# A graph network on one core: VectorE, not GpSimd, puts the next block's gather indices in place

## What is computed

```
k, q, v = typed_linear(x, ntype, Wk / Wq / Wv)          # one of 3 matrices by the node's type
a  = sum(att[etype] applied to k[src] * q[dst]) * pri / sqrt(32)      # per edge and head (4 heads of 32)
w  = softmax of a over the edges with the same dst
h  = segment_sum(msg[etype] applied to v[src] * w, dst)
x  = typed_linear(h, ntype, Wa) * alpha + x * (1 - alpha)
```

## Time and profile before

| | |
|---|---|
| time, median of 3 runs | 7933.0 us (7932.73 to 7936.94) |
| span of the profiled execution, first to last instruction | 9921.5 us |
| gathers L443 | 4160, busy 3981.4 us, 957 ns each |
| copies L439 on POOL | 130, 219 ns each |
| busy share of the span: PE, DVE, POOL, ACT | 56%, 47%, 46%, 41% |

### The profile page before, as it was taken

How to read it: one execution, slowest core, us unless ns; L and a number is a source line. 1 busy time by engine, 2 the same in 40 slices (tenths; PEclk the granted TensorE clock), 3 DMA queues, 4 the chain that set the end, 5 groups by cost and what they waited for, 6 DMA issues and landing times.

```text
span 9921.5 us, 147395 instructions
## 1 busy us (share of the span) xinstructions
PE 5554.4 (56%) x33354; PEld 4735.9 (48%) x33355; DVE 4643.5 (47%) x12764; ACT 4066.5 (41%) x10084; POOL 4557.4 (46%) x4797
## 2 busy tenths in 40 slices
PE   5654545586554555955555559445454594555554
PEld 3544444464444444744444447344444573444443
DVE  5254545532555555235554552355555523555555
ACT  1244444432444444324444443344444433444442
POOL 0345555433455554335555542445555424555553
PEclk9866676797677666977666679767767796676667
DMA  2322222213222221232222213222222132222221
GB/s 69 144 62 70 70 71 70 68 70 125 69 71 72 71 72 56 100 107 72 69 72 72 69 45 124 93 69 71 70 70 71 37 140 83 73 74 73 73 76 36
DMA packets 272656, 761.00 MB, mean 77 GB/s; under 512 B 87871, under 2 KB 104356, under 8 KB 271908
## 3 DMA queue, kind: packets, MB, share of 16 engines
q0 software_dynamic: 199680, 545.53, 19.2%
q1 hardware_dynamic: 72228, 208.51, 5.4%
HBM read 557.87 MB, written 195.88 MB: 76 GB/s over the span
## 4 chain that ended last, share of the span: by engine, by line
PE 31%; another core or an unknown queue 25%; DVEq 16%; issue 12%; DVE 10%; POOLq 3%; ACT 2%; ACTq 1%; DMA 0%; POOL 0%; SPq 0%
PE ps L535 6%; PE ps L627 6%; DVEq L1061 5%; DVEq L1051 5%; PE ps L643 4%; PE ps L648 4%; PE ps L552 3%; POOLq L459 3%; DVEq L228 2%; PE ps L555 2%; PE ps L588 1%; PE ps L642 1%; DVE prod L1045 1%; DVE wmsg L1025 1%
## 5 line engine op out<-in xcount | busy, mean ns | idle before, releaser
L443 POOL DMA_INDIRECT rows<-table,idx_now x4160 | 3981.4, 957 | 3529.5 <-DVE wmsg L1029 1878.9
L642 PE MATMUL ps<-zeros,identb 128*128 128x132 bf16 x2080 | 555.0, 267 | 3189.9 <-DVE wmsg L1029 2780.9
L704 ACT ACTIVATE prod<-iota_n,dloc 128x128 bf16<-128x128 f32 x6240 | 1988.9, 389 | 106.0 <-issue 78.7
L642 PEld LDWEIGHTS ps<-zeros,identb 128*128 128x128 bf16 x2080 | 242.1, 116 | 3353.3 <-issue 3171.5
L1045 DVE TENSOR_TENSOR prod<-ps,rows 128x512 f32<-128x512 f32 x1040 | 715.5, 688 | 2352.6 <-remote 1820.4
L709 ACT ACTIVATE ohf<-prod,ones 128x512 f32<-128x512 bf16 x1040 | 750.5, 722 | 2326.4 <-remote 1887.0
L627 PE MATMUL ps<-qn,ohT 128*128 x8320 | 1583.6, 350 | 67.8 <-issue 62.7
L627 PEld LDWEIGHTS ps<-qn,ohT 128*128 128x128 f32 x8320 | 1407.3, 255 | 135.9 <-issue 129.7
L643 PE MATMUL ps<-wmsg,ohf 128*128 128x132 f32 x4160 | 1267.6, 398 | 0.0
L648 PE MATMUL ps<-wmsg,ohf 128*128 128x132 f32 x4160 | 1090.9, 355 | 0.0
L588 PE MATMUL ps<-identb,oh 128*128 128x128 bf16 x4160 | 531.8, 268 | 730.4 <-ACT ohT L721 358.8
(11 more groups left out here) (162 smaller groups left out, 6391.4 us busy)
## 6 DMA issues: line engine op xcount, KB each, us to landing
table<-rows SPq DMA_DIRECT2D x245, 768.0 KB, 3.2
rows<-table,idx_now POOLq DMA_INDIRECT x4160
out<-h SPq DMA_DIRECT2D x1, 3072.0 KB
wk<-in_L_gnn_Wk SPq DMA_DIRECT2D x20, 48.0 KB
wq<-in_L_gnn_Wq SPq DMA_DIRECT2D x20, 48.0 KB
wv<-in_L_gnn_Wv SPq DMA_DIRECT2D x20, 48.0 KB
wa<-in_L_gnn_Wa SPq DMA_DIRECT2D x20, 48.0 KB
attw<-in_L_gnn_rel_att SPq DMA_DIRECT2D x20, 24.0 KB
```

What stands on the lines that cost most here:

```text
L443: pool.indirect_dma_start(out=rows[:, slot, j, :], out_offset=None, in_=table, in_offset=bass.IndirectOffsetOnAxis(ap=idx_now[:, half, c:c ...
L642: pe.matmul(bank[:, AW:2 * AW], identb[:], zeros[:], start=True, stop=True)
L704: act.activation(squares[:, turn % 2, j * P:(j + 1) * P], iota_n[:], ACT.Square, bias=dloc[:, at(4 * q + j)], scale=-1.0)
```

## The change

At the first quad of a layer POOL copies 64 columns, both halves of `idx_now`, and drains once. For blocks 2 to 25 VectorE copies the 32 columns: in slot 2 of block n, behind L1029, it writes those of block n+1 to the other half and raises a new semaphore `indices_ready`. POOL waits for that semaphore before the first gather of blocks 2 to 25. It is 24 copies a layer on DVE, 120 in all, and one copy with a drain a layer on POOL where there were 26.

```
@@ -180,6 +180,7 @@
         s_gath = [sem(f"gathered{i}") for i in range(RING)]
+        s_idx = sem("indices_ready")
@@ -435,9 +436,11 @@
                     half = slot // BQ
-                    if slot % BQ == 0:
-                        pool.tensor_copy(idx_now[:, half, :], idx[:, at(4 * q, BS)])
+                    if is_first(q):
+                        pool.tensor_copy(idx_now[:], idx[:, 0:2 * BS].rearrange("p (a c) -> p a c", a=2))
                         pool.drain()
+                    if slot % BQ == 0 and not is_first(q, RING):
+                        hold(pool, s_idx, l * (BLOCKS - 2) + n - 1)
                     for j in range(4):
                         c = 4 * (slot % BQ) + j
                         pool.indirect_dma_start(
@@ -1027,6 +1030,8 @@
                         dve.tensor_copy(wmsg[:, b, :, D:AW], w).then_inc(s_wm, 1)
+                    if slot % BQ == 2 and not is_first(n) and not beyond(n + 1, BLOCKS):
+                        dve.tensor_copy(idx_now[:, 1 - slot // BQ, :], idx[:, at((n + 1) * BS, BS)]).then_inc(s_idx, 1)
                     if b == 1 and not beyond(q + 2):
```

## The result

The changed kernel takes 7484.0 us (median of 4 runs, 7473.97 to 7490.11), the kernel before 7934.97 us (median of 4, 7932.73 to 7936.99). The ratio on record is 0.9428, with a 95% interval of 0.9417 to 0.9440 (the two medians alone give 0.9432). It is faster by 451 us, where 420 had been forecast. The profiled execution has a span of 7482.8 us, so this time profile and metric agree.

What follows compares the result with a forecast made beforehand. It took POOL's queue to bound the edge stages in timed runs. Per block -3.7 + 0.1 + 0.1 = -3.5 us, times 120 = -420, took 7933 to 7513, rounded to 7515 us; range 7450 to 7760.

Steps and rivals of the forecast that it cites:

- POOL's queue as the bound: Edge stages: in timed runs POOL's queue of gathers, copies and drains sets their time.
- 1188 us a layer: POOL's work in an edge stage: gathers 1046, boundaries 92, last gather to last weighting 50 us.
- the 1988.5 us: Profiled span over timed median, 9921.5 against 7933.0 us; put down to remote DVE waits absent from timed runs.
- 3.7 us a boundary: POOL at block boundaries: copy with drain delays the next gather by 3.7 us, 25 times a layer.
- 24 boundaries, since the first is covered: POOL per layer: the boundary into block 1 gains nothing, with 16 slots free; 24 gain, 120 in all, 444 us.
- 0.2 us a block held back: Loss per block: 0.1 us for lengthened gathers, 0.1 us for gathers and DVE waiting for each other.
- 1086 us a layer: DVE and PE chain in the edge stages: its low bound, with no remote waits.
- rival 1: DVE's chain takes over early, remote waits partly remaining: 7715 us, range 7570 to 7880, chance 0.22.
- The added copy: DVE, slot 2: 120 copies of 128x32 at 0.2 us, 24 us in all, beside the gathers while POOL bounds.
- the estimated 298 us: Port contention by the Trainium skill: 120 copies cost up to 298 us, result near 7810; the prediction doubted that size.
- What would show it: Signs: timed median falls about 420 us, profile span stays 9921 within 100, POOL's rest grows from 2038.1 to near 2450.
- its own sign: Whole profile: the prediction counts as wrong if the profile's span falls with the time.

Runs made afterwards that it cites:

- e1: The kernel before the change, unedited, profiled a second time: 7946.19 us, profile span 7944.4 us.
- e4: Changed kernel with a POOL drain put back at the boundaries into blocks 1 to 25 of each layer, copy left on VectorE: 7935.82 us, ratio 0.9989.
- e7: Changed kernel with three gathers a quad instead of four, zeros in the fourth place: 7085.36 us, ratio 0.8925.
- e3: Changed kernel with one POOL drain put back at the boundary into block 1 of each layer: 7499.85 us, ratio 0.9438.
- e6: Changed kernel with five index copies on VectorE instead of one, four into an unused tile: 7469.45 us, ratio 0.9407.
- e8: Changed kernel with L1032, the small copy of the weights, written as a product with ones: 7473.63 us, ratio 0.9412.
- e10: Changed kernel with softmax weights read from PSUM, so L1028 has one input there, and L1007 dropped: 10081.44 us, ratio 1.0178, on chip 14.
- e9: Changed kernel with L1028 split into four operations of 128x128: 10086.36 us, ratio 1.0181, on chip 14.
- e11: Changed kernel with two POOL drains in a row at the 125 boundaries: 9867.75 us, ratio 0.9959, on chip 14.
- e2: The changed kernel, unedited, run again on chip 13: 7485.76 us, ratio 0.9422.
- e5: Changed kernel with the 120 copies back on POOL, a block ahead, with a semaphore and no drain: 7490.61 us, ratio 0.9431.

## Why the prediction was right, and where it was not

**POOL's queue as the bound.** Right. The account of 1188 us a layer for POOL's work against 1190.7 was the step that carried it; in e1 the five stages have a mean of 1193 us, and POOL never waits over 0.3 us for a slot. That the sum came so close is in part luck: the mean gather is 970 ns and not 957, some 11 us a layer more, and from the last gather to the last weighting it is 43.5 us and not 50 (7735.9 to 7779.4 in e1). e4 and e7 show it by experiment: POOL's time put back comes back whole, POOL's time taken away is gained until another chain holds.

**Where the 1988.5 us came from.** Here the prediction had the right conclusion from a wrong reading. It took the excess for something "on top" that the profile has. e1 was profiled without it, and on chips 14 and 9 all runs had it: 9907.06 and 9920.19 us. On chips 13 and 10 none had it. None of these chips was used twice, so whether it belongs to the chip or to the time is not shown; the chip of the first profile is not on record. Where it occurs this program is 25% slower, with a granted TensorE clock of 0.74 instead of 0.82 over the run and long waits for TensorE that the profile can name no releaser for. It is not the gathers that are late: of the 182 times that DVE stood idle for over 3 us before L1045 in the first profile, the packets of the quad's gathers had landed 3.8 us or more before in every case (at 3077.3 for the L1045 at 3105.36). Nor does the clock alone account for it: TensorE is busy 5554.4 us there and 5253.7 in e1, 301 us of the 1977. What stalls there is open. The name "remote" says little, for in that profile many semaphore events are missing: it has no time to landing for the gathers, where e1's has 2.8 us.

**3.7 us a boundary.** 3.6 by e4 and by the timeline of e1, a term 3% too large. The median of the drain, 3.679 us, was no support for it: in e1 the same row has 15.074.

**24 boundaries, since the first is covered.** Wrong, by reading the start of the stage in a trace where POOL rested 32 us behind it. e3 puts 2.8 us on each of the five first boundaries by the times, 3.6 by the trace. With 125 in place of 120, and 3.6 us each, the sum is 450, and the measured gain 451.

**0.2 us a block held back** for lengthened gathers and for two chains in balance, 24 us. Neither came: the mean gather is 970 ns in e1 and 968 after the change. These 24 us and the five boundaries (18), less the 12 by which 120 x 3.7 was too large, are the 30 us by which the gain was above the forecast. The chain is not at 1086 us a layer but at 1024 (e7). Taking the remote waits off the slow execution did not undo all of its slowness, for its ordinary waits were longer too: 293.0 us for L627, where e1 has 96.5. So there were 76 us of room under POOL's 1100, and rival 1 was further off than its chance of 0.22 said.

**The added copy.** 0.173 us, hidden behind the waits for gathers, as expected; even five of them are (e6). Contention of the copy with gathers: no loss was found, and nothing of the estimated 298 us. What the prediction put down to L1025 and L1029 together is L1025's (e8 to e10).

**What would show it.** The gathers across a boundary and the wait for `indices_ready` came out as said. The profile's span and POOL's growing rest did not, and could not: both assumed that every profile has the long waits. By its own sign, a profile whose span falls with the time, the prediction would have counted as wrong; it was the sign that was wrong, not the bound. Whether the change gains anything where the kernel before takes 9907 us was not run, so the 5.7% hold for the other condition alone. e9 and e10, the changed kernel with another L1028 and no drains, lost 1.8% there, e11 with its drains gained 0.4%; no run separates the two edits.

No version was found that beats the changed kernel beyond its scatter by an edit whose reason was shown. e6 and e8 were 16 and 12 us faster than e2, on another chip, and the intervals of the ratios overlap.

## What to carry to other kernels

An engine that issues gathers can be the bound while it is busy 58% of the span (POOL in e1; in its edge stages 68%): count its issues by their start-to-start distance, add what stands between them, and hold the sum against the stage. A drain behind a queue of gathers waits for them, here for 3.6 us; put what it protects a block ahead, behind a semaphore, and on whichever engine. And hold the span of a profile against the timed runs before reading its waits: if they differ, take another profile before explaining either, and note the chip of each.

## What the runs showed of the hardware

- The same kernel took 7944.29 us on one chip and 9907.06 on another, with 15 runs on each that agree within 0.7%. The granted clock over the run was 0.82 and 0.74; in the first edge stage 0.78 [e1] and, in the slow first profile, 0.69.
- A gather of 128 rows of 1 KB holds POOL for 0.946 us and 0.30 more. A copy of 128x32 fits into the 0.30 (e5: 1.33 us from gather to gather).
- A gather that starts 0.05 to 0.5 us into an fp32 product of two SBUF tiles (128x512, 0.69 us) ends 0.82 us behind the end of that product; with the product split in four, or one input in PSUM, the longest gather is 1.15 us instead of 1.46.
- A second drain behind the first is recorded with 0.047 us, the first with 3.613 (e11); a boundary with one drain costs 3.6 us (e4).
